# Two more memsets in each pause on GpSimd between the scatters of the last stage

## The reference, cut to what matters

```
expert_weights, top_experts = jax.lax.top_k(scores, TOP_K)          # 2 of 8 experts for each of 4096 tokens
slot = jnp.where(valid, bin_ids * capacity + offsets, E * capacity)  # capacity 1024
xb = jnp.zeros((E * capacity + 1, hs), x.dtype).at[slot].set(xf[src])
h = jax.nn.gelu(jnp.einsum('ech,ehf->ecf', xb, w1))
y = jnp.einsum('ecf,efh->ech', h, w2).reshape(E * capacity, hs)
out = jnp.zeros((T, hs), x.dtype).at[src].add(flat_w[order][:, None] * yv)
```

## Time and profile before

| | us |
|---|---|
| median of 3 runs | 971.59 |
| lowest and highest | 971.56, 973.98 |
| the profiled execution's own time | 973.98 |
| its span, first to last instruction | 972.2 |
| PE busy | 908.6 (93%) |
| DVE busy | 703.1 (72%) |
| ACT busy | 635.8 (65%) |
| POOL busy | 362.8 (37%) |

### The profile page before, as it was taken

One profiled execution on the slowest core, in us unless ns is written; L12 is line 12 of the kernel. 1 busy time (PEld: TensorE's weight loads), 2 busy tenths in 40 slices (PEclk: granted clock), 3 DMA queues, 4 the chain that ended last, 5 costly groups with the idle time before them and its releaser, 6 DMA issues.

```text
span 972.2 us, 17832 instructions
## 1 busy us (share of the span) xinstructions
PE 908.6 (93%) x6484; PEld 650.3 (67%) x6484; DVE 703.1 (72%) x1857; ACT 635.8 (65%) x1097; POOL 362.8 (37%) x412
## 2 busy tenths in 40 slices
PE   5597988998999999999999999999999998999997
PEld 3354644554667887767777777776777565899983
DVE  8978786777669787586877868687885866873324
ACT  4477768776798667667767677777776565464430
POOL 4347053114000101251554517355371515068771
PEclk9689998998999999999999999999999999899999
DMA  5844335346214233301111111110110413023317
GB/s 130 233 121 113 96 101 131 95 107 190 87 34 112 67 110 85 95 22 44 66 42 44 47 44 44 44 62 27 54 55 28 168 46 106 2 76 94 113 49 238
DMA packets 86179, 83.15 MB, mean 86 GB/s; under 512 B 8978, under 2 KB 72456, under 8 KB 86092
## 3 DMA queue, kind: packets, MB, share of 16 engines
q1 hardware_dynamic: 80868, 73.33, 26.2%
q0 software_dynamic: 4320, 8.27, 2.5%
q10 hardware_dynamic: 904, 0.42, 0.1%
HBM read 50.54 MB, written 31.72 MB: 85 GB/s over the span
## 4 chain that ended last, share of the span: by engine, by line
PE 72%; DVE 18%; ACT 4%; issue 2%; DMA 2%; SPq 1%; POOL 0%; POOLq 0%; DVEq 0%; ACTq 0%
PE psum L1560 19%; PE psum L1602 10%; PE psum L1597 6%; PE psum L1583 6%; PE psum L1396 4%; PE psum L1334 3%; DVE pieces L2097 3%; DVE maxes L1976 2%; PE psum L1350 2%; PE psum L1377 2%; PE psum L1410 1%; PE psum L1517 1%; PE psum L1474 1%; PE psum L1495 1%; PE psum L1304 1%
## 5 line engine op out<-in xcount | busy, mean ns | idle before, releaser
L1560 PE MATMUL psum<-parts,q_stack 128*128 128x512 f32 x640 | 251.9, 475 | 6.8 <-DVE parts L2294 5.7
L2587 ACT ACTIVATE big<-psum,cols 128x512 f32<-128x512 f32 x205 | 139.6, 686 | 80.3 <-PE psum L1560 76.5
L2811 POOL TENSOR_TENSOR hT<-hT,gb_tok 128x512 f32<-128x512 f32 x54 | 77.2, 1430 | 268.5 <-DVE gb_tok L2112 267.8
L1560 PEld LDWEIGHTS psum<-parts,q_stack 128*128 128x128 f32 x640 | 113.0, 191 | 59.9 <-issue 40.9
L1976 DVE TENSOR_REDUCE maxes<-psum 128x4 f32<-128x1024 f32 (+1 forms) x96 | 114.0, 1215 | 20.1 <-PE psum L1350 19.8
L1560 PE MATMUL psum<-parts,k_stack 128*128 128x512 f32 x320 | 126.7, 396 | 0.0
L1602 PE MATMUL psum<-big,ew 128*128 128x512 f32 x234 | 119.4, 594 | 0.0
L1597 PE MATMUL psum<-pieces,w_parts 128*128 128x512 f32 x336 | 97.8, 399 | 0.0
L2891 POOL DMA_INDIRECT routed<-big,slot_i x64 | 66.1, 1033 | 51.9 <-DVE slot_i L2281 30.3
L2097 DVE TENSOR_TENSOR pieces<-big,pieces 128x512 fp32r<-128x512 f32 x88 | 74.1, 847 | 11.4 <-ACT pieces L2594 11.3
L2912 POOL DMA_INDIRECT answers<-hT,to x64 | 62.8, 981 | 45.9 <-DVE hT L2309 29.7
(11 more groups left out here) (430 smaller groups left out, 1930.4 us busy)
## 6 DMA issues: line engine op xcount, KB each, us to landing
gb_tok<-gate_rows SPq DMA_DIRECT2D x32, 512.0 KB, 3.6
q_stack<-q_pieces SPq DMA_DIRECT2D x32, 192.0 KB, 3.5
k_stack<-k_pieces SPq DMA_DIRECT2D x32, 192.0 KB, 4.6
routed<-empty_row SPq DMA_DIRECT2D x4, 1040.0 KB, 7.5
big<-routed SPq DMA_DIRECT2D x16, 260.0 KB, 3.0
answers<-empty_row SPq DMA_DIRECT2D x4, 1024.0 KB, 7.5
q_pieces<-gb_tok SPq DMA_DIRECT2D x16, 192.0 KB, 2.1
k_pieces<-gb_tok SPq DMA_DIRECT2D x15, 192.0 KB, 2.1
```

Source lines behind the costliest of these rows:

```text
L1560: last = eng.matmul(bank(i), w1_part(wp, e)[:, fs], parts[2 * xk + xp][:, :], start=n == 0, stop=n == 2)
L2587: eng.activation(slots[held("slot", "up", n, e, f)], bank(held("bank", "up", n, e, f)), ACT.Relu, bias=col("L0_ffn_b1", e * FC + f)).then_ ...
L2811: eng.tensor_tensor(hT[:, ns], xpT[:, ns] if e == 0 else hT[:, ns], gate_wide[:, e // GHELD % 2, e % GHELD, :], ALU.add).then_inc(sem("acc ...
```

## The change

`pause` clears three tiles in place of one, all of 128 x 256 in bf16, with the semaphore signal on the last. The wait at its head is as before. The planner's costs of a step that has a pause in it go up by 0.5 us.

```
@@ -734,7 +734,7 @@
-                p.step("rt_d", b, m, work=f"pool:{2.9 if (n, m) == (NCH - 1, TPB - 1) else 2.5} dma:1.5", after=[("rt_b", b), ("rt_v", g), ("rt_w", g), *fills, *apart(b)], rank=rank, chain=chain)
+                p.step("rt_d", b, m, work=f"pool:{3.4 if (n, m) == (NCH - 1, TPB - 1) else 2.5} dma:1.5", after=[("rt_b", b), ("rt_v", g), ("rt_w", g), *fills, *apart(b)], rank=rank, chain=chain)
@@ -763,7 +763,7 @@
-        p.step("send", u, work=f"pool:{5.45 if u < RESTED else 5.1} dma:1.5", after=[("ans", u)])
+        p.step("send", u, work=f"pool:{5.95 if u < RESTED else 5.1} dma:1.5", after=[("ans", u)])
@@ -2897,7 +2897,9 @@
             def pause():
                 w.wait_ge(chain.sem, chain.n)
-                eng.memset(mask_qk[:, :, :], 0.0).then_inc(chain.sem, chain.more())
+                for mask in (mask_qk, mask_kq, rows_qk):
+                    last = eng.memset(mask[:, :, :], 0.0)
+                last.then_inc(chain.sem, chain.more())
```

## The result

The changed kernel takes 978.25 us (median of 6 runs, 976.89 to 980.12). The kernel before, run beside it, takes 973.7 us (median of 6, 971.56 to 977.32). The ratio is 1.0055 with an interval of 1.0039 to 1.0072, so the change costs about 5.4 us, between 3.8 and 7.0; the two medians differ by 4.6.

What follows compares the result with a forecast made beforehand. GpSimd's list was taken as the bound from 865.85: 14 pauses at 0.50 us, less 2.1 us of waiting, give 4.9 us, plus 0.9 for the clock: 5.8 us, 971.59 to 977.4; forecast's own range 975.8 to 978.8.

Steps and rivals of the forecast that it cites:

- three waits of 2.1 us in all: GpSimd's true waits for data before unit 12's two columns and unit 13's first: its only cushion from 865.85 on.
- The price of a memset: On GpSimd, two added memsets cost 0.50 us per pause, from memsets starting 0.25 us apart; range 0.40 to 0.68.
- The rival with the durations: Added memsets on GpSimd cost their shown durations, 0.68 us per pause: 7.4 us plus 0.9 for the clock, 979.9; 10%.
- the one with 0.20 per memset: Added memsets on GpSimd cost as little as the present one, 0.40 us per pause: 3.5 us, 975.1; 15%.
- The predicted 4.9: Delay of GpSimd's last transfer: 14 pauses at 0.50 us, 7.0 us, less 2.1 us of waiting.
- The first two pauses: Pauses of units 0 and 1, ahead of 865.85: about 1 us extra, disappearing in GpSimd's 3.88 us wait.
- PE's cover: PE can slip 7.8 us in this stage unseen: unit 15's first column ready at 944.7, GpSimd there at 952.5.
- The ring of four units: DVE's `ans` of a unit needs the unit four earlier landed; unit 11 lands near 936, needed at 944.34: no stall.
- list of signs: Wrong if memset spacing differs from 0.25, GpSimd still waits for DVE before unit 12 or 13, or `ans` waits for landings.
- The clock: Behind the last send, PE idles some 4.7 us, its clock falls, losing 2.4 us less 1.5 slack: 0.9 us.
- The rival in which the clock stays low through all three sums: In the tail, PE's last three sums all run at half clock: 6.1 us more, 982.6; 6%.
- The rival that the pauses are hidden: GpSimd's list is not what its last transfer follows; extra price under 0.36 us per pause, 971.6 to 974.5; 5%.

Runs made afterwards that it cites:

- early: Three memsets in the pauses behind units 2 to 5 only, order as before, against the kernel before: ratio 1.0001 (0.9987 to 1.0015).
- late: Four memsets behind unit 13 and a new pause of four behind unit 14, against the kernel before: ratio 1.0014 (1.0002 to 1.0027).
- no pauses: All 16 pause memsets left out, order as before, against the kernel before: ratio 0.9996 (0.9982 to 1.0010).
- the kernel with the memsets alone: Three memsets in every pause, planner's costs and every engine's order as before, against the kernel before: ratio 1.0054 (1.0035 to 1.0073).
- the two comparisons of times: The full change against the kernel before, measured twice: ratio 1.0055 (1.0039 to 1.0072), then 1.0038 (1.0024 to 1.0051).

## Why the prediction was right

**The bound.** The prediction read that GpSimd's list is the bound from the last routing transfers on, except for three waits of 2.1 us in all. The kernels with early, late and no pauses confirm it piece by piece: ahead of the last wait GpSimd's time can be lost and given back with 0.3 us of effect at most, behind it 1.70 us cost 1.70.

**The price of a memset.** 0.25 us by the distance of starts. The traces have 0.25 everywhere, and sets of 5.80 us where 5.79 was implied. The rival with the durations (+7.4 us up to the last transfer) and the one with 0.20 per memset (+3.5) are both excluded by a stretch of +4.74, and by 90.31 to 90.46 in the five traces with this list of GpSimd (+4.7 to +4.9). The predicted 4.9 is 0.16 too high; the longer transfers account for it, since before one took 1.43 us and after two took 1.01 and 1.15, 0.24 us less over the usual 0.97.

**What hides the rest.** The first two pauses disappeared in the wait for the slot numbers, which shrank from 3.88 to 2.71 us. SP's load of chunk 0 came 3.5 us later in the kernel with the memsets alone, as computed, and the planner's new place for it spared PE the 1.6 us that the old order costs.

PE's cover held, but it was smaller than the prediction said. It read 7.8 us off unit 15. The tightest unit is 13, where GpSimd waits today:

```profile
936.10 1.13 DVE L2309 TENSOR_SCALAR hT<-psum,big 128x128 f32<-128x128 f32 x4 [4.68 <-PE psum L1583]
```

That is the kernel before. DVE starts on unit 13 at 936.10 and GpSimd at 937.23, so every us by which GpSimd starts that unit later is a us of cover and no more: 941.6 - 937.23 = 4.4 by the prediction's own sum, 4.2 measured. PE slipped by 0 in the changed kernel and by 1.8 with the old order, so the error cost nothing.

The ring of four units was also closer than said. The prediction looked at unit 11 alone and found no stall. The unit that is tight is unit 2, the first behind the last routing transfers, and DVE waited for its landing in all six executions with three or four memsets in every pause, for 0.5 to 1.8 us. DVE's idle time took it. By the prediction's own list of signs this was one of being wrong; it was harmless here.

**The clock.** The mechanism was right: idle for 4.3 us where 4.7 was said, a fall 3.6 us behind the stop, a DVE that waits for PE. The size was taken from the one earlier fall, 2.4 us lost; 3.0 were lost here, and DVE ended 1.5 us later in place of 0.9. But the stores took half of that back, a step that the prediction did not have, so that 0.8 us in the tail beside the 0.9 forecast is in part luck. Over many runs the term is too small to be seen. The rival in which the clock stays low through all three sums did not happen: the clock was back at 1.00 after PE had worked for 6.1 us at the low level.

**The sum.** 5.8 us were forecast; 5.6 stand in the traces, and 5.4 and 3.7 us in the two comparisons of times. The second has an interval that ends at 5.0, below the forecast, so the typical cost may be nearer to the 4.7 us of the stretch alone; the two intervals share 3.8 to 5.0. The absolute time came out closer than it deserved: 977.4 was forecast and 978.25 measured, but the kernel before took 973.7 beside it, 2.1 us more than the 971.59 that the forecast started from. The rival that the pauses are hidden gave up to 2.9 us. The first interval excludes that and the second, from 2.3 up, not quite; the stretch of +4.74 and the missing waits do. No kernel run here is measurably faster than the one before.

## What to carry to other kernels

An engine's share of the chain says nothing about its distance from being the bound: GpSimd had 0% of it and 2.1 us to spare over 86 us. Sum the true waits on its list, those above the usual issue gap, and note where the last of them stands. In this kernel work ahead of it was free up to about that sum, work behind it cost in full, and taking work away ahead of it gained nothing. Cover for another engine is to be read at the unit where the last wait stands, not at the last unit.

## What the runs showed that was not expected

The same list of GpSimd takes the same time to 0.15 us in five executions (90.31 to 90.46), while the moment at which this stage begins varies by almost 5 us over all twelve executions (863.4 to 868.2). The spread of the times, 3 to 6 us within each kernel, is of the same size, so it seems to come largely from ahead of this stage; no run looked for where. For a change at the end of a kernel, stretches cut from the trace at a fixed instruction decided what the totals could only bound.

A stall can keep the clock up: with the old order PE lost 1.6 us to a late fetch, ended `keep` that much later, and so was idle for 2.7 us instead of 4.3 before its last sums, and the granted clock stayed at 1.00. The kernel was no faster for it, 1.0054 against 1.0055.
